# Pausing the gathers for the grams: a DLRM interaction kernel on one core

## The chip, the cores and the metric

The kernel runs on one core of one Trainium2 chip. The metric is the device time of one execution in microseconds. The kernel before has a median of 246.88 us over 3 runs (244.02 to 253.89).

## The reference

512 samples, 13 dense features, 26 fields of categories with 6250 rows of 64 floats each. Everything is in float32.

```python
sparse_embed = emb_tables[field_idx[None, :], x_sparse]      # 512 x 26 x 64, gathered
z = sparse_embed.reshape(B, N_FIELDS * K)                    # 512 x 1664
gram = jnp.einsum('bik,bjk->bij', sparse_embed, sparse_embed)
inner = gram[:, iu, ju]                                      # 325 pairs i < j
dnn_in = jnp.concatenate([x_dense, z, inner], axis=-1)       # 512 x 2002
h = relu(dnn_in @ w1 + b1)                                   # w1 is 2002 x 2002
out = sigmoid(h @ w2 + b2)                                   # 512 x 1
```

The indices are clipped to the table (a negative one wraps once) before they are used.

## The kernel before, in words

**Tiles.** The batch is four batch tiles of 128 samples, `bt` 0 to 3. The 2002 inputs stand in 16 tiles of up to 128 rows: 13 tiles (0 to 12) with the embeddings, and three **inner tiles** with the 325 pairs, the dense features and the bias row. The 2002 columns are two halves `h` of 1002 and 1000, each in two chunks of about 500, one PSUM bank each. A **product** is one input tile against one half for one batch tile. It is done in three passes on split operands (`x_hi w_hi + x_hi w_lo + x_lo w_hi`), so it is six matmuls (L1053), three for each chunk. There are 16 x 2 x 4 = 128 products. A **piece** is one tile of one half of `w1` (0.5 MB, L768): SP loads it to one of RAW = 5 buffers, ACT rounds it to `w_hi` (L835), DVE makes `w_lo` (L917), one of HL = 7 places, free again after its last product.

**Phases.** Phase A does batch tiles 0 and 1 with both halves of each `w1` tile; B1 does batch tiles 2 and 3 with half 1; B2 does them with half 0. Each phase ends with the inner tiles.

**Gathers.** GpSimd (POOL) gathers the embeddings with indirect DMAs, 128 rows each (L811), in **groups** of four fields: groups 0 to 5 take four gathers for a batch tile, and the last one (`LAST` = 6, two fields) takes two. `ARRIVALS` lists the 28 groups in their order, k = 0 to 27: 0 to 13 are of batch tiles 0 and 1, 14 and 15 the LAST groups of tiles 2 and 3, and from 16 on groups 0 to 5, each for tile 2 and then tile 3. In all there are 104 gathers. `E` has ER = 5 places, so group k waits until DVE has transposed group k - 5 (L808). After each gather but the first four a small memset (`pace`, L819) marks the progress for SP's first loads. Then DVE transposes (L934), ACT makes `x_hi` (L861), DVE `x_lo` (L947), and both copy the transposed values to `ET` (L866, L952) in the layout of the grams.

**Grams.** The grams of four samples at a time are matmuls of 64 x 64 against 64 x 52 (L1026), in eight **rounds** of 64 instructions in the profile: rounds 0 and 1 are for batch tile 0, 2 and 3 for tile 1, 4 to 7 for tiles 2 and 3 together. A round writes a PSUM slot that a half-done sum has left (`park`: ACT L871 and DVE L956 copy it out), and ACT and DVE copy the round to `G` (L879, L965) before the next one. When all of a batch tile is in `G`, SP takes it to `x_in` (L775 to L796): the pairs between the two halves of the fields by three direct DMAs (`CROSS`, one for each inner tile), the pairs within a half by two stores to DRAM and, when they have landed, two skewed fetches, for inner tiles 1 and 2. Inner tile 0 needs only the first direct DMA. ACT and DVE split them as the others (L853, L947).

**Order.** A planner (`make_orders`, L212) runs once in Python: it goes through `make_todo` (L129), the wanted order of products and rounds, with a length for each operation and writes a fixed order of operations for ACT, DVE, PE and SP. PE may take a step up to AHEAD = 6 ahead of the wanted order. An engine that waits for one operation holds all that stand behind it. In the planned order before, PE does round 0, two products, round 1, four products, round 2, two products, round 3, one product, and then the inner tiles of phase A. DVE has the copies of a round to `G`, the copies to `ET` and the `w_lo` pieces in one line.

**Warmth.** PE begins with WARM = 25 matmuls on a tile of ones (L999), and before product KEEP_AT = 2 it does KEEP = 18 more (L1006), 128 columns each. A float32 matmul stands as two in the profile.

**At the end** a `drain` (DVE L991) applies relu, multiplies with `w2` and sums; ACT applies the sigmoid, and SP stores the output.

The functions of the diff follow as far as they stand in the kernel before.

Of the kernel before, what the change touches and what calls it, by code (L numbers as in the profile page):

```python
# [13 lines left out]
P = 128  # L14
# [4 lines left out]
Q = 32  # L19
# [4 lines left out]
LAST = WIDE  # L24
# [40 lines left out]


BEHIND, GATED = 4, 8
KEEP_AT, KEEP = 2, 18
AHEAD = 6
PATIENCE = 0.5  # L70
ET_REST = 0.13
LOOK = 0.5
SOON = 4
GROUPS = P // 4
PER_BANK = 8
# [15 lines left out]


ET_PARTS = [(LAST, LAST + 1), (0, 3), (3, 5), (5, 6)]

# [32 lines left out]
def make_todo():  # L129


    def a_group(g, bt):
        return [product("A", t, h, bt) for h in (1, 0) for t in GROUP_TILES[g]]

    def b_group(ph, h, g):
        return [product(ph, t, h, bt) for bt in (2, 3) for t in GROUP_TILES[g]]

    def inner(ph, h, bt):
        return [product(ph, t, h, bt) for t in INNER_TILES]

    def gram(bts):
        return [("gram", n) for n, r in enumerate(GRAM_ROUNDS) if {x[0] for x in r} == bts]

    todo = []
    for g in GROUP_ORDER[:-2]:
        todo += a_group(g, 0) + a_group(g, 1)
    (p4, p5), (q4, q5) = [[a_group(g, bt) for g in GROUP_ORDER[-2:]] for bt in (0, 1)]
    inner_0 = inner("A", 0, 0)
    todo += p4 + p5[:3] + q4[:1] + mixed(gram({0}), p5[3:] + q4[1:], per=2)
    todo += q5[:1] + mixed(gram({1}), q5[1:] + inner_0[:1], per=2)  # L150
    todo += inner_0[1:] + inner("A", 1, 0) + inner("A", 0, 1) + inner("A", 1, 1)
    first = [b_group("B1", 1, g) for g in GROUP_ORDER[:2]]
    todo += [s for bt in (2, 3) for f in first for s in f if s[2] == bt]
    todo += b_group("B1", 1, 1) + b_group("B1", 1, 2) + b_group("B2", 0, LAST) + b_group("B1", 1, 3)
    todo += b_group("B2", 0, 0) + b_group("B1", 1, 4) + b_group("B2", 0, 1)
    todo += b_group("B1", 1, 5)
    rest = [s for g in (2, 3, 4, 5) for s in b_group("B2", 0, g)]
    todo += mixed(rest[:9], gram({2, 3}), every=2) + rest[9:]
    todo += inner("B1", 1, 2) + inner("B1", 1, 3)
    todo += inner("B2", 0, 2) + inner("B2", 0, 3)  # L160
    return todo


# [27 lines left out]

INNER_KEYS = [IN_KEY + m for m in range(IT)]

PE_LEN = {"product": 1.38, "gram": 1.5}
ACT_LEN = {"hi": 1.05, "x24": 0.55, "x_hi": 0.43, "evac": 0.36, "park": 0.62}
DVE_LEN = {"lo": 0.70, "turn": 0.46, "x24": 0.60, "x_lo": 0.44, "evac": 0.38, "park": 0.70, "drain": 0.86}
HOP = 0.08
# [14 lines left out]
def make_orders():  # L212
# [50 lines left out]
    def gather():  # L263

        nonlocal pool_at
        while len(e_landed) < len(ARRIVALS):
            k = len(e_landed)
            if k >= ER:
                if ("turn", k - ER) not in done:
                    return  # L270
                pool_at = max(pool_at, done["turn", k - ER] + HOP)
            for _ in range(GROUP_GATHERS[ARRIVALS[k][1]]):
                pool_at += 1.25 if k < 2 else 1.50
                g_issued.append(pool_at)
            e_landed.append(pool_at + (1.3 if k < 2 else 1.9))
# [24 lines left out]
    def update():  # L300
# [34 lines left out]
        for bt in range(BT):  # L335
            for part, (a, b) in enumerate(ET_PARTS):
                at = all_done([("x_lo", bt, g) for g in range(a, b)])
                free = all_done([("gram", n) for b in SPLIT for n in gram_rounds(b)]) if bt >= 2 else 0.0
                if at is not None and free is not None:
                    for op in et_ops(bt, [part]):  # L340
                        for engine in ("act", "dve"):
                            offer_once(engine, op, max(at, free + HOP))
            if bt < 2 or ("moved", bt - 2) in done:
                moved = done.get(("moved", bt - 2), 0.0)
                for n in gram_rounds(bt):
                    if ("gram", n) in done:
                        for op in evac_ops(n, bt):
                            for engine in ("act", "dve"):
                                offer_once(engine, op, max(done["gram", n], moved) + HOP)
            at = all_done([op for n in gram_rounds(bt) for op in evac_ops(n, bt)])  # L350
            if at is not None and ("moved", bt) not in done:
                at = max(at, done.get(("moved", bt - 1), 0.0) - 4.5)
                done["moved", bt] = at + 6.5
                sp_events.append((at + HOP, ("store", bt)))
                sp_events.append((at + 2.8, ("fetch", bt)))
                for m, later in enumerate((4.0, 6.0, 6.5)):
                    offer_once("act", ("x_hi", bt, IN_KEY + m), at + later)
        for c, steps in cells.items():
            at = all_done([("p",) + s for s in steps])
# [242 lines left out]
def build(nc, dense_t, idx, base, emb, w1, w2, b2, out, gram_dram):  # L602
    with ExitStack() as ctx:
# [98 lines left out]
        def landed_count(m):  # L702

            return 32 if m in WITHIN_AT else 16

        def x24_copy(bt, a, h):

            to = X24[64 * h:64 * h + 64, bt % 2, :].rearrange("k (j a s) -> k j a s", j=2, a=2)
            return to[:, :, a, :], T6[64 * a:64 * a + 64, bt % 2, :, h, :]
# [44 lines left out]
        def _(sp):  # L754
            sp.dma_start(x_idx[:, 0:SOON], idx[:, 0:SOON]).then_inc(first_idx_landed, 16)
            sp.dma_start(x_idx[:, SOON:N_GATHERS], idx[:, SOON:N_GATHERS]).then_inc(idx_landed, 16)
            for op in SP_OPS:
                if op[0] == "load":
                    m = op[1]
                    ph, t, h = PIECES[USED[m]]  # L760
                    if EARLY <= m < BEHIND:
                        sp.wait_ge(e_landed[0], 16 * GROUP_GATHERS[ARRIVALS[0][1]])
                    elif BEHIND <= m < GATED:
                        sp.wait_ge(paced, gate_of(m) - SOON + 1)
                    if m >= RAW:
                        sp.wait_ge(w_split, 2 * (m - RAW + 1))

                    sp.dma_start(w_raw[:, m % RAW, 0:HALF_W[h]], w1[t, :, HALF_AT[h]:HALF_AT[h] + HALF_W[h]])\  # L768
                      .then_inc(w_landed[m % RAW], 16)
                if op == ("load", HL + RAW):  # L770
                    sp.dma_start(w2_all[:], w2.rearrange("n o -> (o n)").partition_broadcast(P))\
                      .then_inc(consts_landed, 16)
                    sp.dma_start(b2_all[:], b2.partition_broadcast(P)).then_inc(consts_landed, 16)
                if op[0] == "store":
                    bt = op[1]  # L775
                    rows = Q * (bt % 2)
                    sp.wait_ge(g_copied_act, evac_count("act", rounds_of(bt)))
                    sp.wait_ge(g_copied_dve, evac_count("dve", rounds_of(bt)))
                    if bt == 0:
                        sp.wait_ge(ones_row_ready, 1)  # L780
                    for m, (a, b) in enumerate(CROSS):
                        sp.dma_start(x_in[CROSS_AT[m]:CROSS_AT[m] + HALF * (b - a), bt, m, :],  # L782
                                     G[rows + a:rows + b, HALF:FIELDS, :]).then_inc(x_in_landed[bt][m], 16)
                        if m == 0:
                            for u in (0, 1):
                                within = slice(HALF * u, HALF * (u + 1))
                                sp.dma_start(gram_dram[bt, u].rearrange("(i j) b -> i j b", i=HALF),
                                             G[rows + HALF * u:rows + HALF * (u + 1), within, :]).then_inc(g_stored[bt], 16)
                if op[0] == "fetch":
                    bt = op[1]  # L790
                    sp.wait_ge(g_stored[bt], 32)
                    for m, at in WITHIN_AT.items():
                        skewed = gram_dram[bt, m - 1, 0:WITHIN_ROWS * (HALF + 1), :]
                        sp.dma_start(x_in[at:at + WITHIN, bt, m, :],
                                     skewed.rearrange("(a d) b -> a d b", a=WITHIN_ROWS)[:, 1:1 + WITHIN_COLS, :])\
                          .then_inc(x_in_landed[bt][m], 16)  # L796
            sp.wait_ge(result_ready, 2)
            sp.dma_start(out.rearrange("(p t) o -> p (t o)", t=BT), result[:]).then_inc(out_stored, 16)
            sp.wait_ge(out_stored, 16)
# [2 lines left out]
        def _(pool):  # L802
# [4 lines left out]
            for k, (bt, g) in enumerate(ARRIVALS):  # L807
                if k >= ER:  # L808
                    pool.wait_ge(turned, k - ER + 1)
                for j in range(GROUP_GATHERS[g]):  # L810
                    nc.gpsimd.indirect_dma_start(  # L811
                        out=E[:, k % ER, j, :], out_offset=None, in_=emb_rows,
# [5 lines left out]
                    if at > SOON:  # L818
                        nc.gpsimd.memset(pace[:], 0.0).then_inc(paced, 1)  # L819
                        pool.wait_ge(paced, at - SOON)  # L820

        @block.scalar
        def _(act):
# [172 lines left out]
        def _(pe):  # L996
# [6 lines left out]
            for step in PE_OPS:  # L1003
                if k == KEEP_AT and step[0] == "product":
                    for n in range(KEEP):
                        nc.tensor.matmul(slot[SLOT[1, 1, "all"]][:, 0:P], ones[:], ones[:], start=True, stop=True)  # L1006
                if step[0] == "gram":
                    n = step[1]
                    starts = [bt for bt, rnd, _ in GRAM_ROUNDS[n] if rnd == 0]
# [119 lines left out]
```

## Time and profile before

| what | before |
|---|---|
| median of 3 runs | 246.88 us (244.02 to 253.89) |
| profiled execution | 242.37 us |
| its span, first to last instruction | 240.6 us |
| mean granted TensorE clock | 0.934 |
| PE busy | 214.0 us (89%) |
| DVE busy | 145.8 us (61%) |
| ACT busy | 130.9 us (54%) |
| POOL busy | 123.9 us (52%) |
| HBM read | 37.71 MB, 160 GB/s |

Busy times are sums over one engine's instructions, and the share is of the span. The profile is of one execution, whose time is the span and 1.8 us around it. A matmul's end is modelled. A granted clock of 1.00 is 2.4 GHz and one of 0.50 is 1.2 GHz.

### The profile page before, as it was taken

The page shows a single profiled execution, that of the slowest core. Times are in us where ns is not written, and L with a number is a line of the kernel's source. Part 1 is how long each engine was busy: PE and PEld are TensorE (multiplying, and loading weights), DVE is VectorE, ACT ScalarE, POOL GpSimd, SP SyncE. Part 2 cuts the span into 40 slices and gives each one's busy share as a digit, 9 for nine tenths or more (in the row PEclk, how much of TensorE's full clock was granted, in tenths as well). Part 3 has the DMA queues.
Part 4 walks back from the last instruction along what each step waited for, and adds up shares of the span by engine and source line. Part 5 has one row for each costly group of instructions (what it writes and reads, how often), then busy time and mean ns, then how long its engine had stood idle before and what let it go on. Part 6 is the DMA issues. An engine that isn't in the chain of part 4 may idle for free.

```text
span 240.6 us, 3952 instructions
## 1 busy us (share of the span) xinstructions
PE 214.0 (89%) x1366; PEld 172.7 (72%) x1366; DVE 145.8 (61%) x342; ACT 130.9 (54%) x261; POOL 123.9 (52%) x210
## 2 busy tenths in 40 slices
PE   8999979999999233996599799999999999999994
PEld 8888858777877122684478588888788887887883
DVE  2597375878384200581088396959786878651962
ACT  2584534887395100692087278499688766640201
POOL 5888887878888788068703885888600000000000
PEclk9999999999999855598579999999999999999998
DMA  5676999856575110033127764945897565523000
GB/s 180 185 218 202 344 365 311 249 203 194 194 202 184 25 27 22 5 103 74 29 79 227 242 184 172 260 157 178 280 326 256 151 192 173 177 43 64 11 0 0
DMA packets 15389, 39.02 MB, mean 162 GB/s; under 512 B 3881, under 2 KB 5281, under 8 KB 15369
## 3 DMA queue, kind: packets, MB, share of 16 engines
q1 hardware_dynamic: 11688, 35.27, 45.8%
q0 software_dynamic: 3328, 3.41, 6.6%
q8 instruction: 11, 0.18, 0.3%
q10 hardware_dynamic: 353, 0.08, 0.2%
q14 instruction: 9, 0.07, 0.1%
HBM read 37.71 MB, written 0.69 MB: 160 GB/s over the span
## 4 chain that ended last, share of the span: by engine, by line
PE 62%; issue 9%; POOL 8%; DVE 6%; another core or an unknown queue 5%; DMA 5%; ACT 3%; SPq 2%; DVEq 0%; ACTq 0%; POOLq 0%
PE slot L1053 58%; POOL E L811 7%; PE slot L1026 4%; DMA E<-emb,row_idx 2%; DVE w_lo L917 2%; DMA x_in<-gram_dram 1%; ACT w_hi L835 1%; DVE G L965 1%; SPq L782 1%; DVE x_lo L947 1%; ACT ET L866 1%; DVE ET L952 1%; POOL pace L819 1%; DMA x_idx<-idx 1%
## 5 line engine op out<-in xcount | busy, mean ns | idle before, releaser
L811 POOL DMA_INDIRECT E<-emb,row_idx x104 | 106.3, 1022 | 48.5 <-DVE T L934 19.4
L1053 PE MATMUL slot<-w_hi,x_hi 128*128 128x500 f32 (+6 forms) x256 | 103.8, 405 | 6.3 <-DVE x_lo L947 4.5
L1053 PE MATMUL slot<-w_lo,x_hi 128*128 128x500 f32 (+6 forms) x256 | 101.7, 397 | 0.0
L1053 PE MATMUL slot<-w_hi,x_lo 128*128 128x500 f32 (+6 forms) x256 | 101.5, 396 | 0.0
L917 DVE TENSOR_TENSOR w_lo<-w_raw,w_hi 128x500 fp32r<-128x500 f32 (+6 forms) x128 | 80.5, 671 | 16.2 <-ACT w_hi L835 10.9
L835 ACT CAST w_hi<-w_raw 128x1000 fp32r<-128x1000 f32 (+7 forms) x64 | 65.5, 1029 | 29.1 <-DMA w_raw<-w 12.3
L1053 PEld LDWEIGHTS slot<-w_hi,x_hi 128*128 128x128 f32 (+3 forms) x256 | 49.3, 192 | 20.4 <-DVE x_lo L947 7.0
L1053 PEld LDWEIGHTS slot<-w_hi,x_lo 128*128 128x128 f32 (+3 forms) x256 | 49.4, 193 | 10.8 <-issue 0.6
L1053 PEld LDWEIGHTS slot<-w_lo,x_hi 128*128 128x128 f32 (+3 forms) x256 | 49.5, 194 | 9.4
L866 ACT COPY ET<-T 32x128 f32<-32x128 f32 (+4 forms) x92 | 33.4, 363 | 2.1
L1026 PE MATMUL slot<-ET 64*64 64x52 f32 x512 | 17.8, 235 | 16.2 <-issue 16.2
L1026 PEld LDWEIGHTS slot<-ET 64*64 64x64 f32 x512 | 13.6, 145 | 22.6 <-issue 22.6
L965 DVE COPY G<-slot 26x208 f32<-26x208 f32 x31 | 11.5, 371 | 29.3 <-PE slot L1026 16.4
L879 ACT COPY G<-slot 26x208 f32<-26x208 f32 x33 | 10.7, 324 | 30.9 <-PE slot L1026 18.5
L861 ACT CAST x_hi<-T 128x256 fp32r<-128x256 f32 x24 | 9.7, 405 | 12.7 <-DVE T L934 9.1
L819 POOL MEMSET pace<- 128x64 f32 x100 | 16.6, 166 | 0.1
L947 DVE TENSOR_TENSOR x_lo<-T,x_hi 128x256 fp32r<-128x256 f32 x24 | 10.2, 424 | 8.7 <-issue 5.8
L934 DVE STREAM_TRANSPOSE T<-E 128x256 f32<-128x256 f32 x24 | 10.5, 440 | 6.4 <-DMA E<-emb,row_idx 6.0
L952 DVE COPY ET<-T 32x128 f32<-32x128 f32 (+3 forms) x52 | 12.9, 248 | 1.6
L991 DVE SCALAR_TENSOR_TENSOR slot<-slot,w_all 128x500 f32<-128x500 f32 (+1 forms) x16 | 10.8, 690 | 4.5 <-PE slot L1053 4.3
L947 DVE TENSOR_TENSOR x_lo<-x_in,x_hi 117x128 fp32r<-117x128 f32 (+2 forms) x12 | 3.4, 290 | 12.7 <-ACT x_hi L853 12.7
L999 PE MATMUL slot<-ones 128*128 128x128 f32 x50 | 8.8, 361 | 1.0 <-POOL ones L803 1.0
(33 smaller groups left out, 47.1 us busy)
## 6 DMA issues: line engine op xcount, KB each, us to landing
w_raw<-w SPq DMA_DIRECT2D x32, 501.0 KB
w_raw<-w SPq DMA_DIRECT2D x32, 500.0 KB
E<-emb,row_idx POOLq DMA_INDIRECT x104
w_all<-w SPq DMA_DIRECT2D x1, 1001.0 KB
gram_dram<-G SPq DMA_DIRECT2D x8, 84.5 KB
x_in<-gram_dram SPq DMA_DIRECT2D x8, 42.0 KB
x_in<-G SPq DMA_DIRECT2D x4, 58.5 KB
x_in<-G SPq DMA_DIRECT2D x4, 19.5 KB
```

The lines of the kernel that those rows point to most:

```text
L811: nc.gpsimd.indirect_dma_start(out=E[:, k % ER, j, :], out_offset=None, in_=emb_rows, in_offset=bass.IndirectOffsetOnAxis(ap=row_idx[:, at ...
L819: nc.gpsimd.memset(pace[:], 0.0).then_inc(paced, 1)
L835: nc.scalar.copy(w_parts(m)[0], w_source(m)).then_inc(w_hi_ready, 1)
L866: nc.scalar.copy(*et_copy(bt, part, i, h, half)).then_inc(et_by_act, 1)
L879: nc.scalar.copy(gram_place(bt % 2, s, rnd), gram_view(bt, s, b)).then_inc(g_copied_act, 1)
L917: nc.vector.tensor_tensor(lo[:, cols], w_source(m)[:, cols], hi[:, cols].bitcast(F32), ALU.subtract)\
L947: nc.vector.tensor_tensor(lo, src, hi.bitcast(F32), ALU.subtract).then_inc(x_split, 1)
L952: nc.vector.tensor_copy(*et_copy(bt, part, i, h, half)).then_inc(et_by_dve, 1)
L965: nc.vector.tensor_copy(gram_place(bt % 2, s, rnd), gram_view(bt, s, b)).then_inc(g_copied_dve, 1)
L991: nc.vector.scalar_tensor_tensor(out=acc, in0=acc, scalar=0.0, in1=w2_all[:, at:at + width], op0=ALU.max, op1=ALU.mult, accum_out=parts[:, ...
L1026: last = nc.tensor.matmul(slot[AUX[bt]][64 * c:64 * c + 64, at:at + 2 * FIELDS], e.rearrange("k s f -> k (s f)"), e[:, :, 0:FIELDS], start ...
L1053: last = nc.tensor.matmul(slot[s][:, q * BANK:q * BANK + CHUNKS[h][q][1]], x, w[:, cols], start=(first and m == 0), stop=(end and m == 2))
```

## The change

Five edits; the numbers of the planner's model go with them.

1. **Pause.** GpSimd waits ahead of group k = PAUSE = 16 until `gram_done` is RESUME = 4, that is until rounds 0 to 3 are done. The planner's `gather` has the same wait.
2. **Tile 3 by GpSimd.** The seven DMAs that take batch tile 3's grams to `x_in` are issued by GpSimd after its last gather (`BY_POOL = (3,)`), and SP's list has them no more. The three helpers hold the access patterns that SP had in line.
3. **First inner tile ahead.** In phase A, after batch tile 0's three inner products with half 0, the first inner tile of each of the other three (batch tile, half) pairs comes before their second and third. In phases B1 and B2 all four pairs go so.
4. **Order of phase B.** The B2 groups come one group sooner between the B1 groups, so that twelve B2 products of groups 3 to 5 are left after them, and the rounds 4 to 7 are mixed in after every second of the first ones.
5. **Long matmuls on ones.** Instead of 18 of 128 columns there are 5 of 512 columns, with the ones read four times over.

```diff
-KEEP_AT, KEEP = 2, 18
+KEEP_AT, KEEP = 2, 5
+PAUSE, RESUME = 16, 4
+BY_POOL = (3,)
@@ make_todo
-    todo += inner_0[1:] + inner("A", 1, 0) + inner("A", 0, 1) + inner("A", 1, 1)
+    later = [inner("A", 1, 0), inner("A", 0, 1), inner("A", 1, 1)]
+    todo += inner_0[1:] + [s for steps in later for s in steps[:1]] + [s for steps in later for s in steps[1:]]
...
-    todo += b_group("B1", 1, 1) + b_group("B1", 1, 2) + b_group("B2", 0, LAST) + b_group("B1", 1, 3)
-    todo += b_group("B2", 0, 0) + b_group("B1", 1, 4) + b_group("B2", 0, 1)
-    todo += b_group("B1", 1, 5)
-    rest = [s for g in (2, 3, 4, 5) for s in b_group("B2", 0, g)]
-    todo += mixed(rest[:9], gram({2, 3}), every=2) + rest[9:]
-    todo += inner("B1", 1, 2) + inner("B1", 1, 3)
-    todo += inner("B2", 0, 2) + inner("B2", 0, 3)
+    for n, g in enumerate(GROUP_ORDER[2:]):
+        todo += b_group("B1", 1, g)
+        todo += b_group("B2", 0, GROUP_ORDER[n]) if n < 4 else []
+    rest = [s for g in GROUP_ORDER[4:] for s in b_group("B2", 0, g)]
+    todo += mixed(rest[:7], gram({2, 3}), every=2) + rest[7:]
+    later = [inner("B1", 1, 2), inner("B1", 1, 3), inner("B2", 0, 2), inner("B2", 0, 3)]
+    todo += [s for steps in later for s in steps[:1]] + [s for steps in later for s in steps[1:]]
@@ the planner's lengths
-PE_LEN = {"product": 1.38, "gram": 1.5}
+PE_LEN = {"product": 1.38, "gram": 1.15}
@@ gather
+            if k == PAUSE:
+                if ("gram", RESUME - 1) not in done:
+                    return
+                pool_at = max(pool_at, done["gram", RESUME - 1] + HOP)
@@ update
-                at = max(at, done.get(("moved", bt - 1), 0.0) - 4.5)
-                done["moved", bt] = at + 6.5
-                sp_events.append((at + HOP, ("store", bt)))
-                sp_events.append((at + 2.8, ("fetch", bt)))
-                for m, later in enumerate((4.0, 6.0, 6.5)):
+                if bt not in BY_POOL:
+                    at = max(at, done.get(("moved", bt - 1), 0.0) - 5.0)
+                done["moved", bt] = at + 8.8
+                if bt not in BY_POOL:
+                    sp_events.append((at + HOP, ("store", bt)))
+                    sp_events.append((at + 4.0, ("fetch", bt)))
+                for m, later in enumerate((3.4, 8.4, 8.6)):
@@ build
+        def cross_copy(bt, m):
+            a, b = CROSS[m]
+            rows = Q * (bt % 2)
+            return x_in[CROSS_AT[m]:CROSS_AT[m] + HALF * (b - a), bt, m, :], G[rows + a:rows + b, HALF:FIELDS, :]
...
@@ gpsimd
+                if k == PAUSE:
+                    pool.wait_ge(gram_done, RESUME)
...
+            for bt in BY_POOL:
+                pool.wait_ge(g_copied_act, evac_count("act", rounds_of(bt)))
+                pool.wait_ge(g_copied_dve, evac_count("dve", rounds_of(bt)))
+                for m in range(IT):
+                    nc.gpsimd.dma_start(*cross_copy(bt, m)).then_inc(x_in_landed[bt][m], 16)
+                    if m == 0:
+                        for u in (0, 1):
+                            nc.gpsimd.dma_start(*within_store(bt, u)).then_inc(g_stored[bt], 16)
+                pool.wait_ge(g_stored[bt], 32)
+                for m in WITHIN_AT:
+                    nc.gpsimd.dma_start(*within_fetch(bt, m)).then_inc(x_in_landed[bt][m], 16)
@@ tensor
-                        nc.tensor.matmul(slot[SLOT[1, 1, "all"]][:, 0:P], ones[:], ones[:], start=True, stop=True)
+                        nc.tensor.matmul(slot[SLOT[1, 1, "all"]][:, 0:BANK].rearrange("p (a b) -> p a b", a=4), ones[:],
+                                         ones[:].unsqueeze(1).to_broadcast([P, 4, P]), start=True, stop=True)
```

## Rows read from the trace of the kernel before

**Rows 1.** Busy time by stage: us, each engine's busy (x), clock, DMA, GB/s.

```profile
80.00:125.00 45.00, 29.77 (x306) 21.73 (x307) 14.63 (x42) 14.72 (x39) 26.77 (x48) 0.66 0.19 39
125.00:200.00 75.00, 73.45 (x381) 60.12 (x380) 58.92 (x133) 55.85 (x102) 33.75 (x56) 1.00 0.70 219
```

**Rows 2.** The chain that ended last: start, us, what.

```profile
137.28 59.22 PE slot L1053 x258
...
209.70 27.05 PE slot L1053 x117
```

**Rows 3.** L1026 in one stage (x is the count), then the rounds in the timeline.

```profile
81.00:84.90 3.90, 1.94 (x37) 1.29 (x38) 0.67 0.25 29
...
81.31 0.78 PE L1026 MATMUL slot<-ET 64*64 64x52 f32 x29 [3.25 <-issue]
...
96.11 0.36 PE L1026 MATMUL slot<-ET 64*64 64x52 f32 x2 [0.95 <-issue]
...
102.00 1.50 PE L1026 MATMUL slot<-ET 64*64 64x52 f32 x64
...
109.09 0.69 PE L1026 MATMUL slot<-ET 64*64 64x52 f32 x28
...
118.22 0.77 PE L1053 MATMUL slot<-w_hi,x_hi 128*128 128x500 f32 x1 [0.96 <-issue]
...
123.41 1.18 PE L1026 MATMUL slot<-ET 64*64 64x52 f32 x64
...
196.43 1.18 PE L1026 MATMUL slot<-ET 64*64 64x52 f32 x64
```

**Rows 4.** POOL's gathers: L811 by stage (x is the count), then its timeline.

```profile
0.00:85.20 85.20, 57.96 (x56) 0.98 0.68 216
85.20:97.00 11.80, 7.60 (x8) 0.50 0.13 25
97.00:121.00 24.00, 11.64 (x12) 0.71 0.22 53
...
83.92 0.95 POOL L811 DMA_INDIRECT E<-emb,row_idx  x1 [0.27 <-issue]
...
103.49 0.95 POOL L811 DMA_INDIRECT E<-emb,row_idx  x1 [7.36 <-DVE T L934]
...
130.16 1.20 POOL L811 DMA_INDIRECT E<-emb,row_idx  x1 [10.06 <-DVE T L934]
...
149.30 1.20 POOL L811 DMA_INDIRECT E<-emb,row_idx  x1 [2.00 <-DVE T L934]
...
171.56 1.32 POOL L811 DMA_INDIRECT E<-emb,row_idx  x1 [0.27 <-issue]
```

**Rows 5.** One group from its last gather to x_lo, in the timeline.

```profile
19.88 0.95 POOL L811 DMA_INDIRECT E<-emb,row_idx  x1 [0.27 <-POOL pace L819]
...
22.44 0.45 DVE L934 STREAM_TRANSPOSE T<-E 128x256 f32<-128x256 f32 x1 [1.17 <-DMA E<-emb,row_idx]
...
23.36 0.42 DVE L947 TENSOR_TENSOR x_lo<-T,x_hi 128x256 fp32r<-128x256 f32 x1
```

**Rows 6.** Busy time in two short stages, columns as in rows 1.

```profile
102.00:103.00 1.00, 1.00 (x45) 1.00 (x48) 0.89 (x3) 0.92 (x4) 0.00 (x0) 0.62 0.06 12
118.00:120.00 2.00, 1.78 (x4) 1.49 (x5) 0.00 (x0) 0.00 (x0) 1.73 (x4) 0.50 0.12 24
```

**Rows 7.** Batch tile 1's inner rows, stored and used, in the timeline.

```profile
127.81 0.84 SPq L782 DMA_DIRECT2D x_in<-G  x1
...
137.28 0.50 PE L1053 MATMUL slot<-w_hi,x_hi 123*128 123x502 f32 x1 [1.55 <-DVE x_lo L947]
```

**Rows 8.** The last split of inner rows, in the timeline.

```profile
224.21 0.29 DVE L947 TENSOR_TENSOR x_lo<-x_in,x_hi 111x128 fp32r<-111x128 f32 x1 [0.35 <-ACT x_hi L853]
```

**Rows 9.** The matmuls on ones before product 2, in the timeline.

```profile
13.54 4.18 PE L1006 MATMUL slot<-ones 128*128 128x128 f32 x36
```

**Rows 10.** DVE's copy of the parked sum, in the timeline.

```profile
80.42 0.68 DVE L956 COPY parked<-slot 128x500 f32<-128x500 f32 x1 [4.78 <-remote]
```

More of the change, by code:

```diff
@@ L704, in landed_count, with within_store, within_fetch @@
             return 32 if m in WITHIN_AT else 16
+        def cross_copy(bt, m):
+            a, b = CROSS[m]
+            rows = Q * (bt % 2)
+            return x_in[CROSS_AT[m]:CROSS_AT[m] + HALF * (b - a), bt, m, :], G[rows + a:rows + b, HALF:FIELDS, :]
+        def within_store(bt, u):
+            rows, within = Q * (bt % 2) + HALF * u, slice(HALF * u, HALF * (u + 1))
+            return gram_dram[bt, u].rearrange("(i j) b -> i j b", i=HALF), G[rows:rows + HALF, within, :]
+        def within_fetch(bt, m):
+            at = WITHIN_AT[m]
+            skewed = gram_dram[bt, m - 1, 0:WITHIN_ROWS * (HALF + 1), :].rearrange("(a d) b -> a d b", a=WITHIN_ROWS)
+            return x_in[at:at + WITHIN, bt, m, :], skewed[:, 1:1 + WITHIN_COLS, :]
         def x24_copy(bt, a, h):
@@ L775, in _ @@
                     bt = op[1]
-                    rows = Q * (bt % 2)
                     sp.wait_ge(g_copied_act, evac_count("act", rounds_of(bt)))
@@ L780, in _ @@
                         sp.wait_ge(ones_row_ready, 1)
-                    for m, (a, b) in enumerate(CROSS):
-                        sp.dma_start(x_in[CROSS_AT[m]:CROSS_AT[m] + HALF * (b - a), bt, m, :],
-                                     G[rows + a:rows + b, HALF:FIELDS, :]).then_inc(x_in_landed[bt][m], 16)
+                    for m in range(IT):
+                        sp.dma_start(*cross_copy(bt, m)).then_inc(x_in_landed[bt][m], 16)
                         if m == 0:
                             for u in (0, 1):
-                                within = slice(HALF * u, HALF * (u + 1))
-                                sp.dma_start(gram_dram[bt, u].rearrange("(i j) b -> i j b", i=HALF),
-                                             G[rows + HALF * u:rows + HALF * (u + 1), within, :]).then_inc(g_stored[bt], 16)
+                                sp.dma_start(*within_store(bt, u)).then_inc(g_stored[bt], 16)
                 if op[0] == "fetch":
@@ L791, in _ @@
                     sp.wait_ge(g_stored[bt], 32)
[L792 to L796, printed above, removed]
+                    for m in WITHIN_AT:
+                        sp.dma_start(*within_fetch(bt, m)).then_inc(x_in_landed[bt][m], 16)
             sp.wait_ge(result_ready, 2)
@@ L820, in _ @@
                         pool.wait_ge(paced, at - SOON)
+            for bt in BY_POOL:
+                pool.wait_ge(g_copied_act, evac_count("act", rounds_of(bt)))
+                pool.wait_ge(g_copied_dve, evac_count("dve", rounds_of(bt)))
+                for m in range(IT):
+                    nc.gpsimd.dma_start(*cross_copy(bt, m)).then_inc(x_in_landed[bt][m], 16)
[3 more added lines that the diff above has]
+                pool.wait_ge(g_stored[bt], 32)
+                for m in WITHIN_AT:
+                    nc.gpsimd.dma_start(*within_fetch(bt, m)).then_inc(x_in_landed[bt][m], 16)
         @block.scalar
```

## The prediction, written before the change was timed

> **What bounds the kernel now.** I read the busy time by stage first [rows 1]. From 125 us on PE is busy 73.45 of 75.00 us: nothing is to be had there except by giving PE less work. Between 80 and 125 us it is busy 29.77 of 45.00, at a granted clock of 0.66, with DVE, ACT and DMA nearly empty. That hole is the prize. The chain of waits [rows 2] runs 59.22 us through 258 matmuls without a break (43 products of six, **1.38 us a product**), later 27.05 us without one, and from that one's end the tail is 240.6 - 236.75 = 3.8 us.
>
> The timeline [rows 3] shows what PE does in the hole: gram rounds of 64 matmuls, with "issue" ahead of the pieces, so nothing that the profile can name holds it back. Round 0 starts at 81.31, after 3.25 us of wait behind the parked sums, with 29 matmuls in 0.78 us, and has 37 by 84.9. The other 27 take till 96.47: 15.2 us in all. Round 1 takes 1.50 us. Round 2 starts at 109.09 with 28 quick ones, crawls, and PE's next product comes at 118.22: 9.1 us. Round 3 takes 1.18, and so does round 4, one of four alike. Now POOL beside it [rows 4]: it gathers up to 96.1, stands for 7.36 us, to 103.49, for a transpose of DVE, gathers twelve times up to 120.1, stands to 130.16, and has issued its last gather at 172.88. **The two slow rounds lie under gathers, all six quick ones where POOL stands or is done.** Products are not hurt: the 43 unbroken ones run largely beside gathers. So I read it as gathers slowing how fast PE is fed with instructions: about 60 are waiting (29 matmuls and their weight loads), then a round that wants 128 in 1.2 us gets 54 in 11.6 us (27 matmuls, 84.9 to 96.47), whereas a product wants 12 in 1.38 us.
>
> **The pause.** POOL now waits for gram 3 ahead of group 16. Groups 0 to 15 are 4 x 2 + 12 x 4 = 56 gathers, and 56 is what POOL has issued by 84.87 us [rows 4]. Nothing before that changes, so round 0 still starts at 81.31 under gathers.
> - Round 0. 27 matmuls are left at 84.87: at round 1's pace 0.6 us, at worst the gathers' own landing later (1.6 us, from 20.83 to the transpose at 22.44 [rows 5]). I take the end at 86.0 instead of 96.47: **-10.5 us**, bounds 85.5 and 88.
> - From there to round 2 stood 109.09 - 96.47 = 12.6 us. PE ran six products there, the first two at half clock, and DVE and ACT did the copies to G and ET that the round needs. All hang on round 0's end, so I move them as they are. The clock stood at 0.50 from 85.2 to 97 [rows 4], after PE's idle and thin stretch from 78.06, and rose in 102 to 103 us [rows 6], with full work from 96.5 on; it will be low again from 86 to about 92: half clock is 1.2 GHz, and that is already in the 12.6. Round 2 starts at 98.6.
> - Round 2 takes 1.3 us for 9.1: **-7.8 us**. The two products after it took 118.22 to 123.41 = 5.2 us at a clock of 0.50 [rows 6], since it had dropped under the crawl; without that 2 x 1.38 = 2.8: **-2.4 us**. Round 3 ends at 103.9 for 124.59, **-20.7 us** in all.
>
> What queues behind the new wait: only gathers of tiles 2 and 3 (48 of them), and their readers. Eight of them had been issued before 97 us and twelve more by 121 [rows 4]; now the first goes out at 104.0. One costs 172.88 - 130.16 less the 2.00 us stop at 149.30, through 28, = **1.45 us**. So the last is issued at 104.0 + 48 x 1.454 = 173.8, it lands 1.6 later, and from transpose to x_lo it is 1.3 (22.44 to 23.78): group 27 is ready at 176.8.
>
> Two sums come from this. **By PE:** 240.6 - 20.7 = 219.9, and 218.4 if the 1.55 us wait at 137.28 for the inner rows [rows 7] goes as well, which is what moving the first inner tiles ahead can give. **By POOL:** in the new order 38 of the 64 products of phases B1 and B2 stand before B1 of group 5 for tile 3, so 26 products and 4 rounds wait for group 27: 26 x 1.38 + 4 x 1.1 = 40.3, and 3.8 of tail: 176.8 + 40.3 + 3.8 = **220.9**. PE comes to that product at 103.9 + (1 + 12 + 38) x 1.38 = 174.3, so it wants the group 2.5 us before it is there; that is the new wait. The earlier groups are 4 x 1.45 = 5.8 us apart against 4 products = 5.5 us that each feeds, so PE and POOL run nearly in step throughout. In the old order 34 products stood before that one; the new one takes each B2 group one place sooner, which gives the gathers the time of four products, 5.5 us.
>
> **Inner rows.** Tile 1's rows, stored from 127.81, let PE go on at 137.28, 12.7 us after round 3 [rows 7]. Shifted, tile 1's second inner tile is ready at 116.6. PE has nine products before it from 103.9, 12.4 us, to 116.3: just about covered; at worst (late fetches) up to 2 us, which AHEAD = 6 can fill from phase B.
>
> **Tile 3 by POOL.** Round 7 ended at 209.7, SP issued both tiles' stores and fetches in line, and the last x_lo came at 224.21, 14.5 us later [rows 8]. PE had 20 products then, and now has 17 = 23.4 us, of which 11 (15.2 us) stand before tile 3's second inner tile. POOL is long idle; its seven DMAs cost at most a gather's 1.45 us each, 10.2 us, with one landing in the middle and one at the end (1.6 each): 1.7 + 10.2 + 3.2 + 0.6 = 15.7 at worst, and 12.5 at 1 us each (the first of SP's took 0.84 [rows 7]). I take nothing; at the bad bound 0.5 us. Tile 2's fetches no longer stand behind tile 3's store, also unseen.
>
> **Long matmuls on ones.** 36 of 128 columns took 4.18 us [rows 9], 0.116 each. Ten of 512 columns at four times that are 4.6 us: +0.4 at most, at 14 us, where the next products want gathered groups that come every 5.8 us. Nothing; 0.4 at worst. The planner's other numbers reorder work in slack; 0 to 1 us either way.
>
> The sum is 221 us of span, against 240.6. The profiled execution was 242.37, 1.8 over its span, so 222.8; the median of the runs stood 1.9% above it (246.88), which would make 226.9. The crawl is probably part of that scatter, so I take **225**.
>
> **Rivals.**
> (a) Forecast, 0.66: own range 220 (218.4 + 1.8) to 231 (2 us late in round 0, 2 in inner rows, 1.9% to the median).
> (b) POOL becomes the bound with stops of its own, 0.19. Against it, 56 went out by 85.2 us; for it, after the hole POOL stood 10.06 us for a transpose that DVE's fixed order had late [rows 4]. If such a stop comes back in the resumed gathers, there is no slack of PE over it: 220.9 + 10.1 = 231.0, run 232.8 to 235.
> (c) Only round 2 is mended, 0.07: round 0 had begun badly before the pause, DVE had already taken 2.4 us to see PE's end at 78.05 (idle before L956) [rows 10], and if PE's feed needs as long to recover as the round took, 10.5 us stay: 231.4, run 233 to 236.
> (d) Slower than before, 0.08: gathers are not what starves the grams. Then round 3 still ends at 124.6, and the pause, which costs POOL the 20 gathers it had issued by 121, moves group 27 to 124.7 + 69.8 + 2.9 = 197.4; 40.3 + 3.8 behind it make 241.5, run 243.3, and 248 in the median. It decides on one point, whether round 2 crawls with POOL still. For it: rounds 1 and 3 also differ from 0 and 2 in having begun straight behind busy DVE and ACT; against it, six of six quick rounds have POOL still.
> The Trainium skill speaks for (d): "Runtime: NRT & Kernel Launch", Instruction fetch mechanics, has fetching in the background and says that a block boundary costs "one DMA tail-bump, mostly hidden". By that page gathers could not starve PE, and the sum would be 243.3. This trace does not bear it out for rounds 0 and 2, where PE waited for nothing the profile can name.
>
> This kernel's measurement can tell about 2% from no change, 5 us. (a) to (c) are all below 241.9: faster 0.92. (d) is split over its ends, 0.05 within 2% and 0.03 above. The range, 218 to 236, holds (a), (b) and (c) but for their tails, and leaves (d) out.
>
> **What would show it.** Right: POOL silent from 85.0 to 104; rounds 1 to 3 under 1.6 us each; round 3 ended at 102 to 107; 48 gathers in about 70 us after it; PE unbroken but for 1 to 3 us around 170 to 177; tail 3.8. Wrong in a step: round 0 longer than 6 us (c); a POOL wait for "DVE T" over 2 us after 104 (b); round 2 over 5 us with POOL silent (d); PE waiting for x_lo of inner rows at the end, where tile 3 by POOL is mispriced.

## The result, and the profile after

| what | before | after |
|---|---|---|
| median of 4 runs | 249.12 us (244.02 to 253.89) | 229.03 us (228.26 to 229.78) |
| profiled execution, its span | 242.37, 240.6 us | 228.78, 226.7 us |
| mean granted TensorE clock | 0.934 | 0.985 |

The ratio is 0.933, 95% interval 0.922 to 0.944: faster, inside the range of 218 to 236 and 4 us above the forecast of 225. The ratios here and below leave out executions that lie more than 1.5% above the fastest of their kernel (for the kernel before in experiment 7 they are nine of twelve), so a ratio can differ from that of the medians. But the experiments below found three chips on which the kernel before takes 216 us, and on the one of them where both kernels ran they differ by nothing (1.003, 0.997 to 1.009). So the result has a condition, and the condition is a finding of its own.

The busy time by stage first; it answers to [rows 1].

```profile
80.00:125.00 45.00, 38.40 (x391) 31.23 (x392) 27.88 (x74) 26.41 (x62) 21.15 (x35) 0.92 0.41 120
125.00:200.00 75.00, 69.11 (x534) 55.60 (x533) 55.63 (x122) 51.05 (x92) 44.07 (x72) 1.00 0.62 195
```

The hole between 80 and 125 us is filled but for 6.6 us (PE 38.40 of 45.00, for 29.77), and a new loss stands behind it: PE 69.11 of 75.00 where it had 73.45. The chain of waits (start, us, what) says what both are; it answers to [rows 2] and [rows 3].

```profile
79.08 6.90 issue
85.97 1.10 PE slot L1062 x29
87.22 1.32 PE slot L1062 x35
...
92.56 1.11 PE slot L1062 x64
...
100.68 1.15 PE slot L1062 x64
...
103.59 1.22 PE slot L1062 x64
104.87 0.72 issue
105.59 0.95 POOL E L834
...
165.24 5.35 DMA E<-emb,row_idx
170.61 0.46 DVE T L969
...
172.01 15.30 PE slot L1089 x66
...
199.47 22.99 PE slot L1089 x99
222.48 1.38 DVE slot L1026 x3
```

Round 0 takes 2.6 us for 15.2 and round 2 takes 1.2 for 9.1. Round 3 ends at 104.8 instead of 124.6, and from 105.59 the chain runs through the gathers (POOL has 30% of it, before 8%) until a gather's landing and a transpose at 170.61. Then PE goes unbroken to its end.

The timeline shows the pause, and two things that were not expected: who waits at 79 us, and how long the gathers take afterwards (the second fence is L834's busy time by stage, x its count).

```profile
84.36 0.58 ACT L906 COPY parked<-slot 128x500 f32<-128x500 f32 x1 [7.80 <-remote]
...
85.08 0.68 DVE L991 COPY parked<-slot 128x500 f32<-128x500 f32 x1 [8.42 <-remote]
...
105.59 0.95 POOL L834 DMA_INDIRECT E<-emb,row_idx  x1 [19.50 <-PE slot L1062]
...
165.24 1.41 POOL L834 DMA_INDIRECT E<-emb,row_idx  x1 [0.27 <-issue]
...
177.44 0.97 POOL L834 DMA_INDIRECT E<-emb,row_idx  x1 [0.27 <-issue]
```

```profile
105.50:178.50 73.00, 52.13 (x48) 1.00 0.70 221
```

PE's matmuls are recorded as ended at 79.08, and ACT, which waits for the half before the end, goes on at 84.36, DVE at 85.08: over 5 us late, where [rows 10] had 2.4. POOL is gathering all the while, so this may be another face of the crawl; but it does not always come with it: in experiment 7, where the rounds crawl too, ACT's copy begins at 76.00 and round 0 at 77.92 without a wait.

### The profile page after: what moved, and what is told of

Same layout as the page of the kernel before. It is cut to its first block, busy times and chain, and to the rows that moved or that the text cites. A ratio compares the mean times of both kernels' runs of the same rounds, so it can differ in the third digit from the quotient of the medians.

```text
span 226.7 us, 3899 instructions
## 1 busy us (share of the span) xinstructions
PE 203.4 (90%) x1340; PEld 163.1 (72%) x1340; DVE 146.9 (65%) x345; ACT 129.9 (57%) x258; POOL 133.2 (59%) x217
## 4 chain that ended last, share of the span: by engine, by line
PE 47%; POOL 30%; issue 11%; DMA 6%; DVE 4%; ACT 1%; POOLq 0%; DVEq 0%; ACTq 0%
PE slot L1089 42%; POOL E L834 26%; DMA E<-emb,row_idx 5%; PE slot L1062 5%; POOL pace L842 4%; DVE G L1000 1%; ACT w_hi L870 1%; DMA x_idx<-idx 1%; DVE x_lo L982 1%; DVE slot L1026 1%; ACT x_hi L896 0%; DVE T L969 0%; DVE w_lo L952 0%; ACT result L925 0%; POOLq L830 0%
## 5 line engine op out<-in xcount | busy, mean ns | idle before, releaser
L834 POOL DMA_INDIRECT E<-emb,row_idx x104 | 111.1, 1068 | 48.9 <-PE slot L1062 19.5
L1089 PE MATMUL slot<-w_lo,x_hi 128*128 128x500 f32 (+6 forms) x256 | 100.2, 392 | 0.0
L1089 PE MATMUL slot<-w_hi,x_lo 128*128 128x500 f32 (+6 forms) x256 | 99.9, 390 | 0.0
L870 ACT CAST w_hi<-w_raw 128x1000 fp32r<-128x1000 f32 (+6 forms) x64 | 65.4, 1030 | 32.5 <-PE slot L1089 11.7
L1089 PEld LDWEIGHTS slot<-w_hi,x_lo 128*128 128x128 f32 (+3 forms) x256 | 48.5, 190 | 10.0
L901 ACT COPY ET<-T 32x128 f32<-32x128 f32 (+4 forms) x90 | 32.5, 362 | 2.1
L1062 PE MATMUL slot<-ET 64*64 64x52 f32 x512 | 10.7, 232 | 7.5 <-issue 6.9
L1062 PEld LDWEIGHTS slot<-ET 64*64 64x64 f32 x512 | 9.6, 145 | 10.6 <-issue 9.3
L849 POOL DMA_DIRECT2D x_in<-G x3 | 1.9, 619 | 23.3 <-DVE G L1000 23.3
L1026 DVE SCALAR_TENSOR_TENSOR slot<-slot,w_all 128x500 f32<-128x500 f32 (+1 forms) x16 | 10.8, 689 | 2.3 <-PE slot L1089 2.1
L1034 PE MATMUL slot<-ones 128*128 128x128 f32 x50 | 8.0, 337 | 1.0 <-POOL ones L824 1.0
```

The lines of the kernel that those rows point to most:

```text
L834: nc.gpsimd.indirect_dma_start(out=E[:, k % ER, j, :], out_offset=None, in_=emb_rows, in_offset=bass.IndirectOffsetOnAxis(ap=row_idx[:, at ...
L870: nc.scalar.copy(w_parts(m)[0], w_source(m)).then_inc(w_hi_ready, 1)
L901: nc.scalar.copy(*et_copy(bt, part, i, h, half)).then_inc(et_by_act, 1)
L1026: nc.vector.scalar_tensor_tensor(out=acc, in0=acc, scalar=0.0, in1=w2_all[:, at:at + width], op0=ALU.max, op1=ALU.mult, accum_out=parts[:, ...
L1062: last = nc.tensor.matmul(slot[AUX[bt]][64 * c:64 * c + 64, at:at + 2 * FIELDS], e.rearrange("k s f -> k (s f)"), e[:, :, 0:FIELDS], start ...
L1089: last = nc.tensor.matmul(slot[s][:, q * BANK:q * BANK + CHUNKS[h][q][1]], x, w[:, cols], start=(first and m == 0), stop=(end and m == 2))
```

## The experiments

Every kernel ran beside the kernel before on the same chip. On three chips (experiments 1 to 6) that one took 215.9 to 216.3 us in the median, on a fourth (experiments 7 and 8) 250.8. Which chip gave the result above is not known. Each chip was used on one occasion only, so where I write of a chip that crawls, something else that went with the occasion could be the cause as well.

**1. The pause undone.** The two lines of GpSimd's wait are taken out; the orders stay.

```diff
-                if k == PAUSE:
-                    pool.wait_ge(gram_done, RESUME)
```

> The changed kernel with GpSimd's wait for gram 3 taken out; the fixed orders, the tile 3 DMAs and the long matmuls stay. Theory A (gathers starve PE's feed of instructions, the pause is the whole gain): rounds 0 and 2 crawl again, 9 to 15 us each, round 3 ends near 120 to 126 us for 104.8, and the time is 240 to 250. Rival B (the new orders made the gain): rounds stay under 2.6 us and the time is 227 to 231.

Measured: 214.58 us beside 216.05, ratio 0.995 (0.991 to 0.999). Both theories missed, since neither had the kernel before at 216. L832 (gathers) and L1060 (grams) in the stage of rounds 0 to 3 (busy, count):

```profile
77.00:96.00 19.00, 13.27 (x14) 1.00 0.34 72
```

```profile
77.00:96.00 19.00, 4.72 (x256) 4.24 (x256) 1.00 0.34 72
```

Fourteen gathers, and 256 gram matmuls in 4.72 us beside them, 1.18 a round: on this chip gathers do not starve PE at all. The clock stays at 1.00. It was repeated on two more chips.

> The changed kernel without GpSimd's wait, again. Without the crawl: 213 to 216, up to 1% below the changed kernel. With it: rounds 0 and 2 crawl and it takes 238 to 250, so the pause is the gain; if it stays at 227 to 231 there, the new orders are.

> The changed kernel without GpSimd's wait, a third time, in the hope of a chip that crawls (two have not). Where the kernel before takes 244 to 254: rounds 0 and 2 crawl and it takes 238 to 250, if gathers beside the rounds are the cause there; 227 to 231 if the orders were. Where before takes 213 to 219: 213 to 216, nothing new.

Measured: 214.99 beside 215.87, ratio 1.000 (0.995 to 1.004), and 214.63 beside 216.28, ratio 0.993 (0.988 to 0.997). No crawl in either.

**2. The pause alone,** in the kernel before, in the program and in the planner's `gather`.

> The kernel before with the pause alone, in the program and in the planner. Theory A: round 3 ends at 104 to 107 us as in the changed kernel; the gathers then have 34 instead of 38 products before group 27 is wanted, so PE waits some 3 to 6 us more for gathers: 231 to 236, of the gain of 20 us 13 to 18. Rival B: 245 to 250.

Measured: 222.03 us beside 216.05 (four runs, no interval); so it was repeated.

> The kernel before with the pause alone, for its interval (its first four runs had a median of 222.0 beside 216.1). Where nothing crawls, the pause holds back POOL's gathers 57 and on from about 83 to 96 us and PE waits for them behind unchanged orders: 218 to 223, ratio 1.01 to 1.03. Where the grams crawl: 231 to 236 beside 244 to 254, the pause being most of the gain.

Measured: 220.52 beside 216.28, ratio **1.023** (1.014 to 1.031). Without a crawl the pause is a loss of 4 us: groups 16 to 27 come later, and the old order wants them as early as ever.

**3. Both kernels again,** unchanged.

> The kernel before, once more with a profile. The first experiments found it at 216 us where it had been 249. Theory A2 (the crawl of the grams beside gathers comes with the chip, not with the program): on a chip where it takes 213 to 219, rounds 0 and 2 take 1.2 us each beside gathers; where it takes 244 to 254, they crawl for 9 to 15 us. Rival: rounds crawl in every execution and something else gave 216.

> The changed kernel again. Theory A2: without the crawl the pause frees nothing, and the 20 gathers that it holds back are the price, which the new orders pay back: 214 to 218, ratio 0.99 to 1.01. With the crawl: 227 to 230, ratio 0.92 to 0.94.

Measured, on one chip: 215.03 beside 215.87 (0.997, 0.993 to 1.001) and 216.51 (1.003, 0.997 to 1.009). The rounds of the kernel before there, in the timeline, with the gathers going on beside:

```profile
79.62 1.23 PE L1026 MATMUL slot<-ET 64*64 64x52 f32 x64
...
83.72 1.18 PE L1026 MATMUL slot<-ET 64*64 64x52 f32 x64
...
91.09 1.18 PE L1026 MATMUL slot<-ET 64*64 64x52 f32 x64 [0.53 <-DVE ET L952]
...
95.09 1.20 PE L1026 MATMUL slot<-ET 64*64 64x52 f32 x64
```

Compare [rows 3]: the same program, 15.2 and 9.1 us for the first and third. Up to there both traces agree within 2 us. What the pause costs there is POOL's time. L834's first gather after the pause and the last one of the changed kernel, and then the last one of the kernel before:

```profile
94.47 0.95 POOL L834 DMA_INDIRECT E<-emb,row_idx  x1 [8.78 <-PE slot L1062]
...
165.66 0.95 POOL L834 DMA_INDIRECT E<-emb,row_idx  x1 [0.27 <-POOL pace L842]
```

```profile
156.27 0.95 POOL L811 DMA_INDIRECT E<-emb,row_idx  x1 [0.27 <-POOL pace L819]
```

The last gather is 9.4 us later, and the new orders with their later want of it make good for what in experiment 2, on another chip, was 4 us.

**4. Tile 3 by SP again** (`BY_POOL = ()`).

> The changed kernel with batch tile 3's grams taken to x by SP again. Both theories: the transfers are hidden behind 17 products after round 7, so 228 to 230, no change. If the DMAs on GpSimd did matter, 230 to 234, with PE waiting for x_lo of inner rows after 205 us.

Measured: 215.83 beside 216.05, ratio 1.003 (0.998 to 1.007). The changed kernel had 1.003 too, on another chip: no difference seen.

**5. Short matmuls on ones again.**

```diff
-KEEP_AT, KEEP = 2, 5
+KEEP_AT, KEEP = 2, 18
```

The matmul itself is as before the change, 128 columns.

> The changed kernel with 18 matmuls of 128 columns on ones instead of 5 of 512. If they are only heat: 228 to 230. If fewer PE instructions ahead of the gathered stage matter (52 fewer matmul and load instructions, PE's feed shifted by them): a difference at PE's end of product 43, which after the change came 5.3 us late to ACT and before 2.4 us late to DVE; then round 0 would start nearer 81 to 83 us than 86, and the time be 1 to 4 us shorter.

Measured: 216.95 beside 216.05, ratio 1.008 (1.004 to 1.013). Against the changed kernel's 1.003, on another chip, the intervals overlap. The second question could not be asked where nothing crawls.

**6. One group let through.** The wait ahead of group 16 is for round 1, and a second one ahead of group 17 is for round 3.

```diff
-PAUSE, RESUME = 16, 4
+PAUSES = {16: 2, 17: 4}
...
-                if k == PAUSE:
-                    pool.wait_ge(gram_done, RESUME)
+                if k in PAUSES:
+                    pool.wait_ge(gram_done, PAUSES[k])
```

> The changed kernel with the pause opened for one group: group 16 waits for round 1 instead of 3, group 17 for round 3. Four gathers of 1.39 us go beside the four or five products between rounds 1 and 2. Theory A2: PE's waits for groups 16 and later shrink by up to 5.5 us; without the crawl 1 to 3 us faster than the changed kernel (212 to 215), with it 2 to 5 us faster (223 to 227) if PE's feed recovers when POOL stops, or round 2 crawls again in part (229 to 235) if it doesn't.

Measured: 214.54 beside 215.87, ratio 0.995 (0.990 to 1.000), against 1.003 (0.997 to 1.009) of the changed kernel on the same chip: 2.0 us less in the medians, about 1%, with intervals that overlap. It came on no chip that crawls, so whether PE's feed recovers between two groups was not seen in this form.

**7. No pause, and planned without one.** Experiment 1 with the planner's wait out as well.

```diff
-            if k == PAUSE:
-                if ("gram", RESUME - 1) not in done:
-                    return
-                pool_at = max(pool_at, done["gram", RESUME - 1] + HOP)
```

> The changed kernel without the pause in the program and in the planner, so that the fixed orders of ACT, DVE, PE and SP are planned for gathers that go on. Where nothing crawls: 213 to 215.5, at or below the 214.6 to 215.0 of the kernel whose orders were planned for the pause, and 0 to 1% below the kernel before. Where the grams crawl: 238 to 250.

This one came on a chip that crawls. Measured: 246.63 us beside 250.80 in the medians. The ratio is 1.010 (1.005 to 1.015), on the other side of the medians. All other edits of the change together, without the pause, give 1% of either sign. L1056 (grams) and then L828 (gathers) in the stages of its four rounds:

```profile
77.00:90.00 13.00, 4.92 (x64) 3.06 (x64) 0.66 0.17 27
100.00:103.00 3.00, 1.96 (x64) 1.80 (x64) 0.50 0.00 0
110.00:123.00 13.00, 4.57 (x64) 3.26 (x64) 0.70 0.22 44
125.00:127.00 2.00, 1.30 (x64) 1.18 (x64) 0.87 0.50 110
```

```profile
77.00:90.00 13.00, 9.07 (x10) 0.66 0.17 27
100.00:103.00 3.00, 0.00 (x0) 0.50 0.00 0
110.00:123.00 13.00, 7.53 (x8) 0.70 0.22 44
125.00:127.00 2.00, 0.00 (x0) 0.87 0.50 110
```

Rounds 0 and 2, beside ten and eight gathers, are spread over 11 to 12 us each; rounds 1 and 3, with none, take 1.96 and 1.30.

**8. Every round three times as long.** On that chip too; GpSimd's wait is out.

```diff
-                                last = nc.tensor.matmul(
+                                for again in range(3):
+                                    last = nc.tensor.matmul(
...
```

> The changed kernel without GpSimd's wait, and each gram matmul issued three times over (the same values written again), so a round is 192 matmuls in the profile instead of 64. Rounds 0 to 3 stand beside gathers, 4 to 7 after them, in one execution. If gathers slow PE's feed at all, rounds 0 to 3 are longer than 4 to 7, which should take some 3.4 to 3.6 us; at the crawl's 5 instructions per us they would take 30 us and more. If feeding is untouched, all eight are equal within 0.2 us, and the span is 18 to 20 us above 212.

Measured: 282.29 us, one execution. A round of 192 now outlasts POOL's stretches of gathering, so gathers start and stop **in the middle of a round**. L1061 (grams) and then L832 (gathers), in stages cut where POOL's gathers end:

```profile
88.00:97.70 9.70, 4.64 (x48) 4.22 (x49) 0.50 0.11 25
97.70:104.00 6.30, 6.24 (x144) 6.10 (x143) 0.58 0.01 3
110.80:115.30 4.50, 2.74 (x24) 2.03 (x24) 0.77 0.11 30
115.30:118.00 2.70, 2.46 (x44) 2.29 (x43) 0.50 0.05 11
127.50:133.30 5.80, 2.43 (x19) 1.85 (x19) 0.74 0.14 27
133.30:139.00 5.70, 5.27 (x128) 5.16 (x128) 0.66 0.02 4
```

```profile
88.00:97.70 9.70, 5.70 (x6) 0.50 0.11 25
97.70:104.00 6.30, 0.00 (x0) 0.58 0.01 3
110.80:115.30 4.50, 2.85 (x3) 0.77 0.11 30
115.30:118.00 2.70, 0.00 (x0) 0.50 0.05 11
127.50:133.30 5.80, 3.51 (x4) 0.74 0.14 27
133.30:139.00 5.70, 0.00 (x0) 0.66 0.02 4
```

Three times PE goes from 3 to 5 matmuls per us to 18 to 24 (144 in 6.24 us, 44 in 2.46, 128 in 5.27) when the gathers end. The 48 of the first stage hold a quick start, 34 in 2.54 us; after it there are 14 up to 97.7, 2 per us. The first switch:

```profile
95.31 0.95 POOL L832 DMA_INDIRECT E<-emb,row_idx  x1 [0.27 <-issue]
```

```profile
97.73 6.24 PE L1061 MATMUL slot<-ET 64*64 64x52 f32 x144 [0.97 <-issue]
```

The gather's issue ends at 96.26, and PE runs from 97.73. The opposite switch is in round 1, which begins with POOL still:

```profile
106.83 3.81 PE L1061 MATMUL slot<-ET 64*64 64x52 f32 x124
...
109.46 0.95 POOL L832 DMA_INDIRECT E<-emb,row_idx  x1 [13.04 <-DVE T L967]
...
110.80 0.29 PE L1061 MATMUL slot<-ET 64*64 64x52 f32 x2 [0.16 <-issue]
```

124 matmuls go in 3.81 us; gathers begin at 109.46, and from 110.80 PE gets its matmuls in handfuls, until the gathers end. The same kind of matmul stands on both sides of each switch, in one round, so it is not where in the program a round stands. Nor is it ACT or DVE: across the first switch both stand idle, from 89.8 to 104.0. Round 3 and rounds 4 to 7, with no gathers, take 5.8 us each. I had expected 3.4 to 3.6; a matmul takes 30 ns there against 18 in a round of 64, and why was not tried.

## Why the prediction was right, and where it was off

- **The hole is starved PE, and gathers starve it: right, on chips that crawl.** Experiment 8 shows it within one execution. Not foreseen: that it takes a certain chip, or occasion. Experiment 1 has the same gathers beside the same rounds with no delay.
- **The pause is the gain: supported from both sides, not side by side.** Without it, 246.6 beside 250.8 (experiment 7); with it, 229.0 beside 249.1, and the changed kernel itself did not run on the fourth chip. Which of the other edits shares in the gain on a chip that crawls was not tried.
- **Round 0 to end at 86.0:** it ended at 88.5, 7.9 us earlier than before and not 10.5. I kept its start at 81.31, and it came at 85.97: PE came to it 1.0 us later (79.08 for 78.06) and then waited 6.90 us for the parked sums instead of 3.25, since ACT and DVE began their copies over 5 us late. The row that told of such a wait, [rows 10], stood under rival (c) and not in the sum. The longest part of the term, the crawl past 85 us, is gone as forecast.
- **Round 2 and the clock: right.** 1.2 us for 9.1. The step to round 3 was 3.0 us and not 4.0, since the planner left one product between them instead of two. Round 3 ended at 104.8 for 103.9.
- **POOL becomes the bound, at 220.9: the right mechanism, its sizes too small.** The first gather went out at 105.59 for 104.0, and one cost (178.41 - 105.59) / 48 = 1.52 us for 1.45, so the last one was issued 4.6 us later than 173.8. And a landing was not 1.6 us: the last gather of group 25 was issued by 166.65 and in DVE's hands at 170.61, 4.0 us later, and six others for which DVE stood waiting after the pause took 2.9 to 4.1. Group 25 held PE, not group 27: by my numbers it was ready at 104.0 + 40 x 1.454 + 1.6 + 1.3 = 165.1, and PE went on with it at 172.01. PE waited 1.4 us for it and had 33 products, 4 rounds and the tail left: 33 x 1.38 + 4.6 + 4.2 = 54.3, to 226.3 of 226.7. My landing came from one early row [rows 5], though the page of the kernel before lists 6.0 us of DVE's waits for gathers. PE lost 5.9 us from 125 to 200, nearly all in four waits of 0.9 to 1.9 us, where I had 2.5.
- **No stop of rival (b):** POOL waited for no transpose after the pause. **Rival (c)** is the round 0 term, half true: 2.5 us of its 10.5. **Rival (d)** has the mechanism of the other chips: there gathers starve nothing, and the pause alone costs 2.3%. I had it at 241.5 because I gave it the crawl with another cause; I never asked whether the crawl itself would be there.
- **Instruction fetch in the Trainium skill** ("Runtime: NRT & Kernel Launch", Instruction fetch mechanics): experiments 1 and 3 agree with fetching that is hidden (1.18 us a round beside gathers). In experiments 7 and 8 PE runs dry beside gathers, and no run shows whether fetching is what falls behind there.
- **Tile 3 by POOL: right, nothing** (experiment 4). Round 7 ended at 199.47 and the last inner x_lo at 212.88, 13.4 us later, between my 12.5 and 15.7; POOL's own row:

```profile
209.42 1.27 POOL L855 DMA_DIRECT2D x_in<-gram_dram  x2 [4.62 <-DMA gram_dram<-G]
```

Its stores took 4.62 us of waiting, not 1.6; its seven issues only 4.2 us together.
- **Long matmuls on ones: right.** Ten took 4.45 us for 4.18, off the path.
- **The median:** the sum for the profiled execution was 222.8, and it took 228.78: 6.0 us short, by the gathers and round 0. I scaled 222.8 up to 225 for scatter, and that this hid 2.2 us of it was luck: after the change the four runs lie within 0.7%, so no scaling was due.

**What stays open:** which part of a gather (GpSimd's work for it, or the transfer of its rows) holds PE back, what differs between the chips or the occasions (the gathers' own transfers look alike, 12.2% of the DMA engines' time for 448 packets from 78 to 100 us where the kernel before crawls, 13.2% for 459 where it does not), and whether the change pays on a chip that crawls without its new orders. None of these was tried.

**Which version to keep.** Where nothing crawls, 214.5 with one group let through and 214.6 to 215.0 without a wait are the best seen, 0 to 1% below before. Where the grams crawl, only the change as it is was measured at 229. It cost nothing on the chip without a crawl where it ran, and saved 7% in the comparison above: it is the one to keep, with the two-window pause as the next to try there.

## What to carry to other kernels

A stretch in which PE is fed in handfuls with "issue" between them, while GpSimd gathers, can be a matter of the chip: repeat the kernel before on another chip before the hole is counted as its cost. If the hole is real, small matmuls (128 instructions in 1.2 us here) should stand where GpSimd is still, and long ones (12 in 1.4 us) beside it. And a pause moves the whole train behind it: price what resumes by its most loaded row, for the issue and for the landing, and give it slack in the order of the reader, which here was worth 2% (1.023 with the old orders and 1.003 with the new ones, on two chips).

## What the runs showed of the hardware

- One program took 213.6 to 218.8 us on three chips and 243.7 to 256.5 on a fourth (12 runs). Up to 77 us the trace of the first comparison and that of experiment 3 are alike (PE busy 72.3 and 70.1 us), and then the grams differ: 64 small matmuls in 1.2 us, or in 9 to 15 us beside gathers.
- On a chip that crawls PE got on at 2 to 5 small matmuls per us beside gathers, and at 18 to 24 within 1.5 us of the last one's issue; products of 0.23 us a matmul ran unhurt beside the same gathers [rows 2].
- In the first comparison's trace after the change, ACT went on 5.3 us after the recorded end of PE's last matmul before the rounds (84.36 and 79.08), so the profile's ends are no proof of when a result is there.
- From the end of a gather's issue to DVE it took 1.6 us at 21 us, 1.9 at 178 (177.44 + 0.97 to the transpose at 180.35), and 4.0 at 167 (165.24 + 1.41 to 170.61), with SP's loads of w1 running (the core's DMA engines 0.70 busy from 105.5 to 178.5).
